# A perceiver block on one core: ternary weights turned by DMA, the first rounds and the tail re-ordered

## The chip, the core and the metric

The kernel runs on one core of a Trainium2 chip. TensorE multiplies, VectorE (DVE) and ScalarE (ACT) read its results out of PSUM, GpSimd (POOL) works beside them in SBUF, and SyncE (SP) issues the DMAs in order. The metric is the device time of one execution in microseconds. Before the change it is 314.23 (median of 3 runs, 314.06 to 314.25).

## What is computed

Thirty-two sequences of 64 rows of 512 go through three layers: cross attention with low-rank queries and keys (16 heads, latent width 32), self attention with one head of 128, and a feed-forward layer whose activations are quantized to 4 bits after a Hadamard transform and whose weights are ternary.

```python
x = x + xattn(layernorm(x), ctx, Wq_d, W_qk, Wkv_d, Wv_u)
x = x + attn(layernorm(x), Wqkv, bqkv, Wo, bo)
h = layernorm(x) @ hadamard
s = clip(max(abs(h), -1), 1e-5) / 7            # one step per row
q = clip(round(h / s), -8, 7) * s
scale = clip(mean(abs(w), 1), 1e-5)            # one per output
t = where(w / scale > 0.5, 1, where(w / scale < -0.5, -1, 0)) * scale
x = x + q @ t.T
```

## The kernel before

Two sequences make a pair of 128 rows; there are 16 pairs (0 to 15, N = 15). The work is a software pipeline written out by hand: `body(i, ...)` of each engine does, in round i, the front of pair i+1 (latents, queries, keys, scores), the cross attention of pair i, the self attention of pair i-1 and the feed-forward layer of pair i-2. Rounds -1 to 3 and 12 to 14 are written out, rounds 4 to 11 are a loop, and pairs 13 to 15 end in a tail with an order of its own. Each engine runs its list in the order in which it is written, and waits on semaphores: `made` counts what TensorE has made, `read` what has been read out of PSUM, `done` what VectorE, ScalarE and GpSimd have done. SyncE's list of DMAs is in order too, so a DMA that waits holds those behind it.

The names that matter here:

- `prob`: exponentials of the scores (ACT L385), from `nmx`, the negated maxima (VectorE `largest`, L614 and L618, one call for each half of the heads). TensorE turns them (L957), ScalarE copies them to `prob_t`.
- `latents` copies the latents of the next pair out of PSUM (ScalarE); the projections read them. `x2n` is the normalized input of self attention (GpSimd L314), turned at L1038 and copied to `x2t`; L1046 projects two pairs' queries at once, L1074 and L1078 make queries, keys and values, L1097 the second scores, whose maximum is `second_max` (L644).
- `x3` is turned, copied to `x3t` and multiplied with the Hadamard matrix (L1009) into bank B4. `amax`, `step_raw`, `qinv`, `z` and `qi` quantize that; `qi` are the codes. In the rounds they are turned by a DMA (`codes_by_dma`, behind a small DMA called `gate`), in the tail by TensorE (`quantized_turned`), and `clipped` writes them to `qi_t`. L1156 multiplies them with `tern_t`, VectorE makes `prod`, GpSimd adds `x3` and SyncE stores `res`.
- The ternary weights: `weight_sizes` sums a block of rows' sizes (L585), `weight_scales` makes the thresholds, `ternary(c)` makes block c of `tern` in two operations (L603 `w_neg`, L605). `ternary_transposed` turns two blocks at a time on TensorE (L946), and `ternary_copy` takes them out of PSUM into `tern_t`. Blocks 0 to 2 are made in round 1, block 3 in round 2, and both halves are turned in round 2.
- `keep_busy(n, bank)` issues n matmuls whose result nobody reads. `x2b` is `x2` plus a constant row (GpSimd L328). `hadamard_centred` takes the mean off the Hadamard matrix on GpSimd in round 1.

## Time and profile before

| what | value |
|---|---|
| median of 3 runs | 314.23 us (314.06 to 314.25) |
| the profiled execution, its own time | 315.06 us |
| its span, first to last instruction | 313.3 us |
| mean granted TensorE clock | 0.991 |
| busy: PE, DVE, ACT, POOL | 299.5, 246.9, 208.1, 90.0 us |
| chain that ended last | PE 74%, DVE 11%, ACT 6%, DMA 3% |

The table is of one execution on the profiler. Busy time is an average over stages; the chain of work that ended last says at each place which engine the end waited for. A matmul of 32-bit numbers is recorded as two passes, so a count of passes is twice that of the code's matmuls.

### The profile page before, as it was taken

What the parts mean: (1) busy time and instruction counts of PE and PEld (TensorE: products, weight loads), DVE (VectorE), ACT (ScalarE), POOL (GpSimd) and SP (SyncE); (2) the same over time, 40 slices, a digit from 0 to 9 for tenths busy, and PEclk for the clock granted to TensorE, in tenths of its full rate; (3) what the DMA queues carried; (4) which work ended last, traced back from release to release, by engine and by line L of the source; (5) the groups of instructions that cost most, each with busy time, mean ns of one, the idle gap of its engine ahead of it and who ended that gap; (6) DMA issues with size and microseconds to landing.
All of it is one profiled execution on the core that took longest, in us unless ns stands there. A gap on an engine that the chain in (4) does not pass through costs nothing.

```text
span 313.3 us, 8324 instructions
## 1 busy us (share of the span) xinstructions
PE 299.5 (96%) x3043; PEld 207.5 (66%) x3058; DVE 246.9 (79%) x530; ACT 208.1 (66%) x587; POOL 90.0 (29%) x130
## 2 busy tenths in 40 slices
PE   7997989999999999999999999999999999999993
PEld 6754857667576766768576766768576866648642
DVE  1689798887879878887879878887879878896366
ACT  2578478768596676768596676768596777784400
POOL 2008304140323324051323324051323324141411
PEclk9999799999999999999999999999999999999998
DMA  7995002051311603041310603051311102000001
GB/s 216 376 363 187 4 8 96 19 189 31 106 49 36 186 1 134 17 157 61 108 43 33 184 0 134 17 173 44 110 43 63 26 0 69 19 35 2 33 0 67
DMA packets 20968, 26.94 MB, mean 86 GB/s; under 512 B 10704, under 2 KB 11472, under 8 KB 20944
## 3 DMA queue, kind: packets, MB, share of 16 engines
q1 hardware_dynamic: 20944, 26.62, 26.1%
q8 instruction: 15, 0.25, 0.4%
q14 instruction: 9, 0.07, 0.1%
HBM read 20.71 MB, written 4.19 MB: 80 GB/s over the span
## 4 chain that ended last, share of the span: by engine, by line
PE 74%; DVE 11%; ACT 6%; DMA 3%; SPq 2%; issue 2%; POOL 0%; DVEq 0%; POOLq 0%
PE ps L1009 10%; PE ps L1074 9%; PE ps L957 7%; PE ps L1132 5%; PE ps L1112 4%; PE ps L1078 4%; PE ps L1162 4%; ACT prob L385 4%; PE ps L967 3%; PE ps L1185 3%; PE ps L1156 3%; DMA bo_row<-bo 3%; PE ps L1046 3%; PE ps L1030 2%; DVE mx L614 2%
## 5 line engine op out<-in xcount | busy, mean ns | idle before, releaser
L385 ACT ACTIVATE prob<-ps,nmx,qk_scale 128x128 f32<-128x128 f32 x240 | 89.8, 469 | 34.9 <-DVE nmx L618 34.9
L1009 PE MATMUL ps<-had_s,x3t 128*128 128x512 f32 x104 | 48.2, 605 | 0.7 <-ACT x3t L379 0.7
L614 DVE TENSOR_REDUCE mx<-ps 128x8 f32<-128x1024 f32 x31 | 37.7, 1217 | 7.0 <-PE ps L1132 7.0
L334 POOL TENSOR_TENSOR qk_scale<-aux,power 128x1 f32<-128x1 f32 x16 | 9.3, 580 | 98.4 <-DVE aux L636 98.4
L623 DVE TENSOR_REDUCE sum_a<-prob 128x8 f32<-128x1024 f32 x30 | 35.8, 1210 | 0.0
L379 ACT ACTIVATE prob_t<-ps 128x512 f32<-128x512 f32 x63 | 34.8, 622 | 0.7 <-PE ps L957 0.3
L1009 PEld LDWEIGHTS ps<-had_s,x3t 128*128 128x128 f32 x104 | 18.6, 190 | 24.5 <-issue 22.7
L957 PE MATMUL ps<-ident,prob 128*128 128x128 f32 x240 | 31.8, 276 | 2.1 <-ACT prob L385 2.1
L957 PEld LDWEIGHTS ps<-ident,prob 128*128 128x128 f32 x240 | 26.6, 141 | 5.5 <-ACT prob L385 4.7
L1074 PE MATMUL ps<-x2t,wqkv_s 128*128 128x128 f32 x224 | 28.6, 281 | 0.4
L1074 PEld LDWEIGHTS ps<-x2t,wqkv_s 128*128 128x128 f32 x224 | 26.1, 192 | 2.2 <-ACT x2t L379 1.3
L338 POOL TENSOR_TENSOR res<-prod,x 128x512 f32<-128x512 f32 x13 | 16.5, 1271 | 34.1 <-DVE prod L769 34.1
L1132 PE MATMUL ps<-ckv,q_t 32*64 32x128 f32 x1024 | 19.2, 278 | 0.2 <-ACT ckv L379 0.2
L967 PEld LDWEIGHTS ps<-wv_bd,u_t 128*128 128x128 f32 x112 | 14.6, 192 | 6.9 <-issue 6.2
L311 POOL TENSOR_TENSOR rstd<-aux,power 128x1 f32<-128x1 f32 x14 | 7.7, 548 | 36.7 <-DVE aux L666 36.7
L328 POOL TENSOR_TENSOR x2b<-x,const_row 128x512 f32<-128x512 f32 x14 | 17.8, 1272 | 0.0
L1132 PEld LDWEIGHTS ps<-ckv,q_t 32*64 32x64 f32 x1024 | 15.5, 131 | 2.8 <-issue 0.8
L1112 PE MATMUL ps<-prob_t,ckv_k 128*32 128x256 f32 x240 | 16.1, 385 | 0.3 <-ACT prob_t L379 0.3
L967 PE MATMUL ps<-wv_bd,u_t 128*128 128x128 f32 x112 | 14.8, 276 | 0.5 <-ACT u_t L379 0.5
L1078 PE MATMUL ps<-wqkv_s,x2t 128*128 128x128 f32 x112 | 14.8, 275 | 0.0
L379 ACT ACTIVATE x2t<-ps 128x512 f32<-128x512 f32 x16 | 9.6, 599 | 7.6 <-PE ps L1038 7.2
L1162 PE MATMUL ps<-wo_s,o2t 128*128 128x512 f32 x28 | 14.3, 592 | 0.0
(200 smaller groups left out, 577.1 us busy)
## 6 DMA issues: line engine op xcount, KB each, us to landing
ct<-ctx_cols SPq DMA_DIRECT2D x16, 512.0 KB, 4.8
xt<-x_cols SPq DMA_DIRECT2D x16, 256.0 KB, 2.9
xr<-x_rows SPq DMA_DIRECT2D x16, 256.0 KB, 4.2
y<-res SPq DMA_DIRECT2D x15, 256.0 KB, 2.0
had_s<-hadamard SPq DMA_DIRECT2D x1, 1024.0 KB, 7.7
w_rows<-weight SPq DMA_DIRECT2D x1, 1024.0 KB, 10.7
wqkv_s<-wqkv SPq DMA_DIRECT2D x1, 768.0 KB, 8.4
wqk<-w_qk SPq DMA_DIRECT2D x2, 128.0 KB, 4.3
```

Source lines behind the costliest of these rows:

```text
L379: return nc.scalar.activation(dst, src, ACT.Copy)
L385: last = nc.scalar.activation(prob[:, h, :], ps[:, h // 4, (h % 4) * P:(h % 4) * P + P], ACT.Exp, bias=nmx[:, h:h + 1], scale=qk_scale[:])
L614: V.tensor_reduce(mx[:, h], ps[:, 2 * half:2 * half + 2, :].rearrange("p r (c k) -> p (r c) k", c=EC), AX.X, ALU.max).then_inc(done["mx"], 1)
L623: V.tensor_reduce(sum_a[:, h], prob[:, h, :], AX.X, ALU.add).then_inc(done["sum"], 1)
L957: mm = pe.transpose(ps[:, r, c * P:(c + 1) * P], prob[:, 4 * r + c, :], ident[:])
L967: mm = pe.matmul(ps[:, B1, c * P:(c + 1) * P], u_t[:, c, :], wv_bd[:, c, :], start=True, stop=True)
L1009: mm = pe.matmul(ps[:, B4, :], x3t[:, c, :], had_s[:, c, :], start=(c == 0), stop=(c == EC - 1))
L1074: mm = pe.matmul(ps[:, B1, s * P:(s + 1) * P], wqkv_s[:, c, s * P:(s + 1) * P], x2t[:, c, :], start=(c == 0), stop=(c == EC - 1))
L1078: mm = pe.matmul(ps[:, B2, 0:P], x2t[:, c, :], wqkv_s[:, c, 2 * P:3 * P], start=(c == 0), stop=(c == EC - 1))
L1112: mm = pe.matmul(ps[32 * r:32 * r + 32, B2, :].rearrange("p (c t) -> p c t", c=EC) [:, :, 64 * bb:64 * bb + 64], ckv_k[:, bb, :], prob_t[: ...
L1132: mm = pe.matmul(ps[64 * bb:64 * bb + 64, r, c * P:(c + 1) * P], q_t[g, 1 - par, bb, c, :], ckv[g, 1 - par, bb * SKV:(bb + 1) * SKV], star ...
L1162: pe.matmul(ps[:, B3, :], o2t[:], wo_s[:], start=True, stop=True).then_inc(made["wo"], 1)
```

## The change

- The blocks of `tern` are turned by four DMAs into `tern_t` (`ternary_by_dma`), two issued in round 1 and two in round 2 behind the codes of pair 0. TensorE's transposes and ScalarE's copies of them are gone, and TensorE waits for all four DMAs before the first integer product.
- Round 0 and 1 on VectorE: the last `weight_sizes` moves behind pair 0's second normalization, `ternary(1)` moves ahead of `second_max`, and `ternary(2)` goes to round 2, ahead of `amax`.
- Round 1 on ScalarE and TensorE: `latents` moves behind the exponentials, and six idle-filling matmuls stand ahead of the second half's transposes. Three more are at the start.
- Tail: pair 13's codes are clipped ahead of `second_max`, and its integer product stands ahead of x2's turning, with one filling matmul in place of three. The codes of pair 15 are made, turned and clipped in two halves; `quantizer` is the part of `quantized` ahead of z, with a name of its own.

```diff
+            def ternary_by_dma(c):
+                sp.wait_ge(tern_done, c + 1)
+                sp.dma_start(tern_t[:, :, c * P:(c + 1) * P], tern[:, c, :], transpose=True).then_inc(ternary_turned, 16)
...
+                if pre and 1 <= i <= 2:
+                    for c in range(2):
+                        ternary_by_dma(2 * i - 2 + c)
...
-                if front and not (isinstance(i, int) and i == 0):
+                if front and not (isinstance(i, int) and 0 <= i <= 1):
                     latents()
-                if isinstance(i, int) and i == 2:
-                    ternary_copy(0, B1)
...
+                    if isinstance(i, int) and i == 1:
+                        latents()
...
-                if isinstance(i, int) and i == 2:
-                    ternary_copy(1, 0)
...
                     largest(1, 0)
-                    weight_sizes(3, EC)
                     largest(1, 1)
                 if first and i == 1:
+                    weight_sizes(3, EC)
                     output_bias()
...
                     ternary(0)
                     sums(1)
                     second_query()
+                    ternary(1)
                     second_max()
                     row_variance()
                     row_scale()
-                    ternary(1)
-                    ternary(2)
...
+                    if first and i == 2:
+                        ternary(2)
...
             second_variance(N)
+            clipped(N - 2, B4)
             second_max(N - 1, B3)
-            clipped(N - 2, B4)
             second_sum(N - 1)
...
-            quantized(N, 3, amax_n, floor3_n, step_n, qinv_n)
+            quantizer(N, 3, amax_n, floor3_n, step_n, qinv_n)
+            after(dve, made["qit"], 1)
+            for h in range(2):
+                cols = slice(h * E // 2, (h + 1) * E // 2)
+                V.tensor_scalar(z[:, cols], ps[:, 3, cols], qinv_n[:], ROUND, ALU.mult, ALU.add).then_inc(half_z, 1)
+                dve.wait_ge(half_z, h + 1)
+                V.tensor_scalar(qi[:, cols], z[:, cols], ROUND, QMAX, ALU.subtract, ALU.min).then_inc(half_codes, 1)
             V.tensor_scalar(qscale_n[:], step_n[:], rstd3_n[:], None, ALU.mult).then_inc(done["qscale"], 1)
-            clipped(N, 2)
+            after(dve, made["int"], N - 1)
+            for h in range(2):
+                dve.wait_ge(half_turned, h + 1)
+                V.tensor_scalar(qi_t[:, 2 * h:2 * h + 2],
+                                ps[:, (2, B2)[h], :].bitcast(BF16)[:, 0:E // 2].rearrange("p (c t) -> p c t", c=2),
+                                QMIN, None, ALU.max).then_inc(half_clipped, 1)
             scaled(N - 1)
...
-            keep_busy(1, 0)
+            keep_busy(2, 0)
...
-                        keep_busy(1, 0)
+                        keep_busy(3, 0)
...
-                        if first and i == 2 and c == 0:
-                            pe.wait_ge(read["xo"], 2)
-                            ternary_transposed(0, B1)
...
+                    keep_busy(6, B3)
...
-                if first and i == 2:
-                    pe.wait_ge(read["pt"], i * 4 + 1)
-                    ternary_transposed(1, 0)
...
                 if quant:
+                    if first and i == 2:
+                        pe.wait_ge(ternary_turned, 16 * EC)
                     after(pe, read["qit"], i - 2)
...
             second_scores(N - 1, B3)
-            keep_busy(3, B1)
-            x2_turned(N, 2)
             after(pe, read["qit"], N - 2)
             for c in range(EC):
                 mm = pe.matmul(ps[:, B4, :], qi_t[:, c, :], tern_t[:, c, :], start=(c == 0), stop=(c == EC - 1))
             mm.then_inc(made["int"], 1)
+            keep_busy(1, B1)
+            x2_turned(N, 2)
             p2_turned(N - 1, B3)
...
-            quantized_turned(N, 2)
-            keep_busy(1, B1)
-            after(pe, read["qit"], N)
+            for h in range(2):
+                pe.wait_ge(half_codes, h + 1)
+                for c in range(2):
+                    mm = pe.transpose(ps[:, (2, B2)[h], :].bitcast(BF16)[:, c * P:(c + 1) * P],
+                                      qi[:, (2 * h + c) * P:(2 * h + c + 1) * P], ident_b[:])
+                mm.then_inc(half_turned, 1)
+                keep_busy(1, B1)
             for h in range(2):
                 for c in range(EC):
+                    if h == 0 and c % 2 == 0:
+                        pe.wait_ge(half_clipped, c // 2 + 1)
```

VectorE at the end of round 1, before: from the second scores' maximum of pair 0, behind the copy of the next queries, to the maximum of pair 2's first scores. In brackets stands what an operation waits for.

```order
L644 TENSOR_REDUCE mx<-ps 128x1 [waits made_s2]
L646 TENSOR_SCALAR nmx<-mx 128x1 [waits done_mx2]
L628 BN_STATS stat<-xr 128x6 [waits made_lat,ld_xr0]
L631 BN_AGGR mv<-stat 128x2 [waits done_stat1,ld_wq]
L636 TENSOR_SCALAR aux<-mv 128x1 [waits done_qk_scale,done_mv1]
L603 TENSOR_SCALAR w_neg<-w_rows,w_nhalf 128x512 [waits tern_done,whalf_done]
L605 SCALAR_TENSOR_TENSOR tern<-w_rows,w_half,w_neg 128x512 [waits neg_done]
L603 TENSOR_SCALAR w_neg<-w_rows,w_nhalf 128x512 [waits tern_done,whalf_done]
L605 SCALAR_TENSOR_TENSOR tern<-w_rows,w_half,w_neg 128x512 [waits neg_done]
L747 RECIPROCAL rsum<-sum_a 128x16 [waits done_xm,done_sum]
L751 RECIPROCAL rsum<-sum 128x1 [waits done_exp2]
L614 TENSOR_REDUCE mx<-ps 128x8 [waits made_s]
```

And after:

```order
L604 TENSOR_SCALAR w_neg<-w_rows,w_nhalf 128x512 [waits tern_done,whalf_done]
L606 SCALAR_TENSOR_TENSOR tern<-w_rows,w_half,w_neg 128x512 [waits neg_done]
L645 TENSOR_REDUCE mx<-ps 128x1 [waits made_s2]
L647 TENSOR_SCALAR nmx<-mx 128x1 [waits done_mx2]
L629 BN_STATS stat<-xr 128x6 [waits made_lat,ld_xr0]
L632 BN_AGGR mv<-stat 128x2 [waits done_stat1,ld_wq]
L637 TENSOR_SCALAR aux<-mv 128x1 [waits done_qk_scale,done_mv1]
L749 RECIPROCAL rsum<-sum_a 128x16 [waits done_xm,done_sum]
L753 RECIPROCAL rsum<-sum 128x1 [waits done_exp2]
L615 TENSOR_REDUCE mx<-ps 128x8 [waits made_s]
```

Block 1 (w_neg and tern) has moved ahead of the second scores' maximum, and block 2 has left this place.

VectorE in round 2, around the quantizer's maximum, before and then after:

```order
L712 TENSOR_SCALAR aux<-mv 128x1 [waits done_mv3]
L715 TENSOR_REDUCE amax<-ps 128x1 [waits made_had]
L603 TENSOR_SCALAR w_neg<-w_rows,w_nhalf 128x512 [waits tern_done,whalf_done]
L605 SCALAR_TENSOR_TENSOR tern<-w_rows,w_half,w_neg 128x512 [waits neg_done]
L722 TENSOR_SCALAR step_raw<-amax,floor 128x1 [waits done_floor3,done_amax]
```

```order
L712 TENSOR_SCALAR aux<-mv 128x1 [waits done_mv3]
L604 TENSOR_SCALAR w_neg<-w_rows,w_nhalf 128x512 [waits tern_done,whalf_done]
L606 SCALAR_TENSOR_TENSOR tern<-w_rows,w_half,w_neg 128x512 [waits neg_done]
L717 TENSOR_REDUCE amax<-ps 128x1 [waits made_had]
L604 TENSOR_SCALAR w_neg<-w_rows,w_nhalf 128x512 [waits tern_done,whalf_done]
L606 SCALAR_TENSOR_TENSOR tern<-w_rows,w_half,w_neg 128x512 [waits neg_done]
L724 TENSOR_SCALAR step_raw<-amax,floor 128x1 [waits done_floor3,done_amax]
```

Block 2 now stands between aux and amax, block 3 where it stood.

SyncE from the rows of pair 2 to the first store, before and then after:

```order
L219 DMA xr<-x_rows 128x512 [waits read_xo]
L215 DMA ct<-ctx_cols 128x1024 [waits made_lat]
L219 DMA xr<-x_rows 128x512 [waits read_xo]
L223 DMA gate<-bqkv 16x1 [waits done_qi]
L224 DMA_TRANSPOSE codes<-qi 128x4x128
L228 DMA y<-res 128x512 [waits done_res]
```

```order
L220 DMA xr<-x_rows 128x512 [waits read_xo]
L224 DMA_TRANSPOSE tern_t<-tern 128x4x128 [waits tern_done] x2
L216 DMA ct<-ctx_cols 128x1024 [waits made_lat]
L220 DMA xr<-x_rows 128x512 [waits read_xo]
L228 DMA gate<-bqkv 16x1 [waits done_qi]
L229 DMA_TRANSPOSE codes<-qi 128x4x128
L224 DMA_TRANSPOSE tern_t<-tern 128x4x128 [waits tern_done] x2
L233 DMA y<-res 128x512 [waits done_res]
```

Blocks 0 and 1 are turned behind the rows' load of round 1, and blocks 2 and 3 behind the codes.

## Rows read from the trace of the kernel before

**Rows 1.** Windows of 1 us: window, length, busy time by engine, granted clock, DMA.
```profile
30.00:31.00 1.00, 0.39 (x4) 0.39 (x5) 0.97 (x6) 1.00 (x4) 0.58 (x3) 1.00 1.00 395
...
33.00:34.00 1.00, 1.00 (x10) 1.00 (x12) 0.96 (x2) 1.00 (x3) 0.72 (x1) 0.50 0.00 0
```

**Rows 2.** Timeline of TensorE, round 1: start, length, operation, idle before.
```profile
30.61 1.21 PE L957 MATMUL ps<-ident,prob 128*128 128x128 f32 x8 [2.08 <-ACT prob L385]
31.79 1.12 PE L1038 MATMUL ps<-ident,x2n 128*128 128x128 f32 x4
32.84 2.08 PE L1046 MATMUL ps<-lat,wqk 64*128 64x128 f32 x16
```

**Rows 3.** Chain that ended last, rounds 2 and 3: start, length, what.
```profile
46.49 1.10 PE ps L1009 x2
47.59 0.45 PE ps L946 x8
...
72.90 1.09 PE ps L1046 x16
```

**Rows 4.** Timeline, end of round 1 (VectorE, and TensorE's scores of pair 2).
```profile
38.11 0.23 DVE L644 TENSOR_REDUCE mx<-ps 128x1 f32<-128x64 f32 x1 [2.11 <-PE ps L1097]
...
39.54 0.49 DVE L603 TENSOR_SCALAR w_neg<-w_rows,w_nhalf 128x512 f32<-128x512 f32 x1
...
39.89 1.20 PE L1132 MATMUL ps<-ckv,q_t 32*64 32x128 f32 x64
...
40.06 0.75 DVE L605 SCALAR_TENSOR_TENSOR tern<-w_rows,w_half,w_neg 128x512 bf16<-128x512 f32 x1
...
42.30 1.21 DVE L614 TENSOR_REDUCE mx<-ps 128x8 f32<-128x1024 f32 x1
```

**Rows 5.** Timeline, round 2 (VectorE and ScalarE).
```profile
44.41 0.68 DVE L651 TENSOR_TENSOR xm<-ps,rsum 128x512 f32<-128x512 f32 x1
...
48.07 1.02 ACT L379 ACTIVATE tern_t<-ps 128x1024 bf16<-128x1024 bf16 x1 [0.48 <-PE ps L946]
...
49.59 0.15 DVE L712 TENSOR_SCALAR aux<-mv 128x1 f32<-128x1 f32 x1
...
50.70 0.69 DVE L715 TENSOR_REDUCE amax<-ps 128x1 f32<-128x512 f32 x1 [0.97 <-PE ps L1009]
...
51.31 1.01 DVE L603 TENSOR_SCALAR w_neg<-w_rows,w_nhalf 128x512 f32<-128x512 f32 x1
...
54.25 0.43 DVE L729 TENSOR_SCALAR qi<-z 128x512 bf16<-128x512 f32 x1
...
57.09 0.30 ACT L472 ACTIVATE p<-ps,nmx 64x64 f32<-64x64 f32 x1
```

**Rows 6.** The codes' transposing DMA (timeline, and view of tile codes), and TensorE's integer product.
```profile
55.10 1.30 SPq L224 DMA_TRANSPOSE codes<-qi  x1
...
60.43 0.81 PE L1156 MATMUL ps<-tern_t,qi_t 128*128 128x512 bf16 x3
```
```profile
L224 SPq DMA_TRANSPOSE codes<-qi x13: 1188/1195/1297, 55.1 to 266.4; - x13
...
DMA to landing us min/median/max: 2.4/2.4/2.5
```

**Rows 7.** Timeline of the tail.
```profile
288.80 0.60 ACT L379 ACTIVATE x2t<-ps 128x512 f32<-128x512 f32 x1 [0.35 <-PE ps L1168]
...
289.57 1.06 PE L1202 MATMUL ps<-x2t,wqkv_s 128*128 128x128 f32 x8
...
305.84 0.75 DVE L821 TENSOR_SCALAR z<-ps,qinv_n 128x512 f32<-128x512 f32 x1
...
307.54 0.42 DVE L830 TENSOR_SCALAR qi_t<-ps 128x512 bf16<-128x512 bf16 x1 [0.37 <-PE ps L1168]
...
308.71 1.26 POOL L364 TENSOR_TENSOR res<-prod,x 128x512 f32<-128x512 f32 x1 [8.18 <-DVE prod L848]
...
309.29 0.96 DVE L903 TENSOR_TENSOR res<-prod_n,x 128x256 f32<-128x256 f32 x1
...
310.68 0.42 DVE L903 TENSOR_TENSOR res<-prod_n,x 128x256 f32<-128x256 f32 x1
```

25 lines of the change are left out of this document (6 added, 19 removed).

## Prediction

> **What bounds the kernel now.** I read the chain that ended last first, then the engines' timeline of the stretches that the change touches, then granted clock by microsecond. The middle of the kernel is one chain of matmuls, round after round, and nothing in it is touched; so what is won or lost before round 3 is carried to the end unchanged, and the change is worth what it does to rounds 1 and 2 and to the tail. Three things stand in the way there. First, TensorE sits idle for 2.08 us ahead of the second half of pair 1's transposes [rows 2], and then its granted clock is 0.50, the lower of its two levels (1.2 GHz against 2.4), where it had been 1.00 [rows 1]: the paired projection's 16 passes take 2.08 us there and 1.09 in round 3 [rows 2, 3]. Second, VectorE makes two ternary rows at 39.54 to 42.2, one at 40.06 and another behind it, and so starts the maximum of pair 2 at 42.30, although the scores that it reads (1.20 us from 39.89) had ended at 41.09 [rows 4]. Third, round 2 has the ternary weights' transposes in TensorE's row ahead of the last Hadamard passes, ScalarE's copy of them (1.02 us, once for each half), and a VectorE that waits 0.97 us for the Hadamard product and only then makes the last ternary row [rows 5].
>
> **Round 1, clock.** Six more idle-filling matmuls (0.11 us for each of their twelve passes, about 1.3 us) fall into the gap of 2.08 us. ScalarE does the copy of the latents behind the exponentials rather than between them, so these end some 0.4 us sooner; the gap that is left is about 0.4 us. The gap that brought the clock down was five times that, so I take the clock to stay at its upper level. The turning of x2 still waits for GpSimd, since GpSimd's work ahead of it is untouched; it starts at 31.79 as before [rows 2]. From there: four transposes at full clock, about 0.45; the projection 1.09 instead of 2.08; then queries, keys, values in 2.8. The second scores would be there at about 36.4 instead of 38.1, 1.7 us sooner.
>
> **Round 1, VectorE.** Its row is serial up to the copy of the queries; what follows had waited 2.11 us when it started at 38.11 [rows 4], so the copy ended at 36.0; the weight size moved to behind aux2 takes 0.68 us there, but the same amount is swallowed where the first comparison (w_neg) waited for GpSimd's x2b, so I take 0 for it (at worst 0.68 later). Behind the queries now comes ternary row 1: 0.49 + 0.75 + 0.03 between them [rows 4] = 1.27, to 37.3. The second scores' maximum started at 38.11 [rows 4] and can start at 37.3: 0.81 sooner, with TensorE no longer what it waits for. The two exponentials, the ckv copy and the scores of pair 2 follow: 39.89 - 0.81 = 39.1, end 40.3. VectorE has no ternary row left there, is free at 38.8, and takes the maximum at 40.3 instead of 42.30: 2.0 us gained. What is late next is that wait for the scores.
>
> **Round 2.** The six exponentials and x3's copy follow that maximum: the Hadamard product starts at 46.49 - 2.0 = 44.5 [rows 3]. It loses the eight transposes that stood in it (0.45) and so has ended by 48.2, not 50.7. VectorE, however, gains less: its next operations wait for the output and attended matmuls behind the scores, which came only 0.81 sooner, so xm moves from 44.41 to 43.1 (1.3) [rows 5], and with it all that follows on VectorE and GpSimd; aux3 ends at 49.74 - 1.3 = 48.4 [rows 5]. Ternary row 2 now goes into the place of the 0.97 us wait: 1.27, to 49.7; amax 0.69, to 50.4. The comparison of row 3 took 1.01 us instead of 0.49 because x2b held it [rows 4, 5]; x2b is 1.3 sooner too, so it ends 1.3 sooner, and the codes (qi) end at 54.68 - 1.3 = 53.4.
>
> The shared lock shows in the rows: 1.01 against 0.49 of the same comparison [rows 4, 5], and in the tail 0.96 against 0.42 [rows 7]. The Trainium skill (SBUF — State Buffer, "SBUF: two separate sides") says the same, that VectorE and GpSimd share one port pair, held by one of them for a whole instruction; by that rule the 0.68 us of the moved weight size would be hidden as I took it.
>
> **The transposes by DMA, where the forecast is decided.** Ternary rows 0 and 1 go at 34 and 37.3, with over 20 us to spare. Rows 2 and 3 stand in SyncE's queue behind the codes of pair 0, so they can't leave before qi is done, although the rows themselves are ready at 49.7 and 51.8. Codes: issue at 55.10 - 1.3 = 53.8, 1.30 us on the queue, 2.4 us to landing [rows 6]. If each one follows as soon as the queue has issued the one ahead, the third is issued at 53.8 + 2.6 = 56.4 and lands at 58.8. The integer product needs it; it started at 60.4 [rows 6]. TensorE by itself would be there at 58.35: the codes end at 53.4, the sums take 1.2, the second maximum 0.4, so the exponentials of p start at 55.05 instead of 57.09 [rows 5], 2.05 sooner; the copy of the ternary halves (1.02 each) is gone from ScalarE, so it is not in the way. So the landing is last, by 0.45, and the product starts at 58.8: **1.6 us gained**. No row shows a transposing DMA queued behind another. Its price lies between the 1.2 to 1.3 us of an issue and the 2.4 us of a whole one [rows 6]; I take 1.3, since the destination engines were busy for only half a microsecond of the 2.4. The two ends give 58.35 (TensorE's own) and 61.0.
>
> A rule speaks against the edit. The Trainium skill (VectorE: DVE Perf Modes, "Rules for kernel authors") says to transpose a 128x128 block on TensorE if PSUM will do, and its table "The three transpose paths" prices the DMA path at 1309 ns for a block of bfloat16. These instructions turn four blocks each; by that price, added up, three of them would take 15.7 us and end at 69.5. The trace disagrees: four blocks land in 2.4.
>
> **Tail.** Pair 13's integers are made ahead of x2's turning. The matmuls then fall where three filling ones stood, but the queries of pair 15 wait for ScalarE's copy of x2t anyway, 288.80 + 0.60 = 289.40 against a start at 289.57, with one weight load of 0.1 before it [rows 7]: 0.05 gained. The last codes in halves: z, at 305.84, takes 0.75 whole; a half can't take under 0.38 and I estimate 0.48, and 0.30 for half of the 0.43 of qi [rows 5, 7]. Four half steps and their hand-overs end at 307.39, where the whole codes ended at 307.05. The transposes of the second half are two instead of four, and the second clip ends at about 308.04 instead of 307.96 [rows 7]. The product of pair 14 stands behind it, GpSimd's sum behind that (from 308.71, 1.26 us) and the end behind GpSimd: the first half of the last sum takes 0.96 instead of 0.42 and ends 0.28 after GpSimd [rows 7]. So the end moves by +0.08. The integer matmuls gain nothing. Both together: 0.03 later, bounds -0.2 and +0.4. The start's filling matmuls lie in waits for loads: 0.
>
> **Sum.** The profiled execution took 315.06 (span 313.3, 1.76 around it). 315.06 - 1.6 + 0.03 = 313.5. The median of the runs lies 0.83 under the profiled one: 312.7.
>
> **Rivals.** (a) The transposes are not what comes last, because they queue closer than 1.3 us or qi is sooner: product at 58.35, gain 2.05: 312.2. For it: the DMA engines are hardly busy. Against: the issue alone is 1.2 to 1.3. (b) The clock falls all the same, at 31.5: then the second maximum stays at 38.11 and the scores of pair 2 at 39.89; only the ternary row behind it is gone, 1.2 us at the maximum, 0.5 at xm and about 0.5 at qi, third landing at 59.6: gain 0.8, 313.5. For it: filling leaves a gap of 0.4 and another of 0.4 ahead of x2. (c) The gain is swallowed before round 3 by a wait not seen here, such as VectorE's longer row: 314.2. (d) Slower: each transposing DMA waits until the one ahead has landed. Then the third lands at 53.8 + 3 x 2.4 = 61.0, 0.6 later than the product started, and the tail adds its 0.03: 314.9. It decides from a spacing of 2.1 us on ((60.4 - 2.4 - 53.8) / 2). Against it: the DMA engines' short work in each.
>
> **How the numbers follow.** Forecast 0.53, (a) 0.17, (b) 0.12, (c) 0.10, (d) 0.08. A difference under 0.2% (0.63 us) is about what a measurement of this kernel can't tell from none; (b) lies on the near side of that line for two parts in three. Faster 0.79, same 0.13, slower 0.08. The range goes from (a) with a little of the tail's bound, 311.9, to beyond (b), 313.9; (d) and half of (c) are left out.
>
> **What would show it.** Granted clock 1.00 from 28 to 36 us; second maximum at 37.3; maximum of pair 2 at 40.3; qi of pair 0 ending at 53.4; three transposing DMAs 1.3 us apart and TensorE waiting for the last some 0.4 us before the integer product at 58.8; rounds 3 on in the same lengths as before; the last sum still held by GpSimd. I am wrong if the clock falls, if the third transposing DMA lands later than 60.4, or if VectorE's row in round 1 isn't done by 37.3.

## The result: slower by 0.6%

| version | median, us | lowest to highest | runs |
|---|---|---|---|
| before | 314.24 | 313.55 to 315.74 | 20 |
| changed | 316.08 | 314.55 to 318.01 | 20 |

The ratio is 1.0059, with a 95% interval of 1.0039 to 1.008. The forecast was 312.7 with a range up to 313.9, so it is wrong in sign and by 3.4 us. The runs of the changed kernel spread over 3.5 us, those of before over 2.2. The spread of the changed kernel has a pattern: ten of the twenty executions have a mean granted TensorE clock of 0.993 or less and a median of 317.6, the other ten have 0.996 or more and a median of 315.0. The profiled one took 317.7 and is of the first ten, so it shows a loss of 2.6 us where the medians show 1.8.

The profiled execution has a span of 315.9 (before 313.3) and a mean granted clock of 0.992 (before 0.991): there is again one fall of the clock, but in another place. Place by place, along the steps of the prediction:

**Start.** TensorE's timeline of the changed kernel, then that of the kernel before (start, length, engine, line, operation, count). The passes of the same code take 1.81 instead of 1.22, and the first scores come 2.4 us later; a part of it are the added fillers.

```profile
0.98 2.93 PE L925 MATMUL ps<-mean_w 128*128 128x128 f32 x12 [0.98 <-POOL power L293]
...
3.70 1.81 PE L932 MATMUL ps<-wq_raw,mean_w 128*128 128x64 f32 x8
...
9.03 1.08 PE L1003 MATMUL ps<-ct,wkv_s 128*32 128x256 f32 x8
...
12.46 1.20 PE L1130 MATMUL ps<-ckv,q_t 32*64 32x128 f32 x64 [0.17 <-ACT ckv L387]
```
```profile
3.70 1.22 PE L916 MATMUL ps<-wq_raw,mean_w 128*128 128x64 f32 x8
...
7.08 0.64 PE L996 MATMUL ps<-ct,wkv_s 128*32 128x256 f32 x8 [0.52 <-DMA ct<-ctx_cols]
...
10.06 1.20 PE L1132 MATMUL ps<-ckv,q_t 32*64 32x128 f32 x64 [0.17 <-ACT ckv L379]
```

By the maximum of pair 1's first scores (24.19, before 22.91) 1.28 us of that is left. So the times of rounds 1 and 2 are compared from there. (VectorE's first `weight_sizes` stands ahead of this maximum in both kernels; the moved one stands behind it.)

**Round 1.** The changed kernel again: TensorE, the windows that answer to [rows 1], and VectorE.

```profile
30.52 1.50 PE L925 MATMUL ps<-mean_w 128*128 128x128 f32 x12
31.86 1.04 PE L964 MATMUL ps<-ident,prob 128*128 128x128 f32 x8
32.84 0.65 PE L1042 MATMUL ps<-ident,x2n 128*128 128x128 f32 x4
33.42 1.16 PE L1050 MATMUL ps<-lat,wqk 64*128 64x128 f32 x16
```
```profile
30.00:31.00 1.00, 1.00 (x12) 1.00 (x11) 1.00 (x4) 1.00 (x5) 1.00 (x2) 1.00 0.81 301
33.00:34.00 1.00, 1.00 (x14) 0.83 (x15) 1.00 (x1) 0.47 (x1) 1.00 (x2) 1.00 0.68 262
```
```profile
38.13 0.22 DVE L645 TENSOR_REDUCE mx<-ps 128x1 f32<-128x64 f32 x1
...
41.14 1.23 DVE L615 TENSOR_REDUCE mx<-ps 128x8 f32<-128x1024 f32 x1 [1.31 <-PE ps L1130]
```

The six fillers fill the gap, the clock stays at 1.00, and the paired projection's 16 passes take 1.16 where [rows 2] has 2.08. The second scores' maximum starts at 38.13 with no idle time before it: VectorE's own row is what it waited for, as forecast. The maximum of pair 2 starts at 41.14, before 42.30 [rows 4]: 1.16 sooner by the clock on the wall, 2.44 counted from the late start.

**Round 2.** VectorE, SyncE's queue, then the chain that ended last, in the changed kernel and in the kernel before.

```profile
51.03 1.13 DVE L604 TENSOR_SCALAR w_neg<-w_rows,w_nhalf 128x512 f32<-128x512 f32 x1
...
54.09 0.43 DVE L731 TENSOR_SCALAR qi<-z 128x512 bf16<-128x512 f32 x1
```
```profile
54.93 1.19 SPq L229 DMA_TRANSPOSE codes<-qi  x1
56.16 2.58 SPq L224 DMA_TRANSPOSE tern_t<-tern  x2
```
```profile
57.47 3.77 DMA tern_t<-tern
61.25 0.05 issue
61.29 1.52 PE ps L1156 x4
62.81 1.71 PE ps L1162 x2
64.52 1.24 PE ps L974 x8
...
67.79 3.63 PE ps L1016 x8
```
```profile
60.43 0.81 PE ps L1156 x3
61.24 0.86 PE ps L1162 x2
62.10 0.89 PE ps L967 x8
...
65.20 3.63 PE ps L1009 x8
```

The last step of the codes starts at 54.09, before 54.25 [rows 5], and ends at 54.52 (before 54.68). The three transposing DMAs are issued at 54.93, 56.16 and 57.47, 1.2 and 1.3 apart, as forecast. The third lands 3.8 us after its issue and not 2.4, at 61.24. TensorE waits for it and then runs the next three groups in 4.47 instead of 2.56 us (one of the four passes of before's integer product isn't in its record):

```profile
61.29 1.52 PE L1156 MATMUL ps<-tern_t,qi_t 128*128 128x512 bf16 x4 [2.17 <-DMA tern_t<-tern]
```
```profile
60.00:61.00 1.00, 0.00 (x0) 0.00 (x0) 0.14 (x1) 0.82 (x3) 0.00 (x0) 1.00 0.06 7
61.00:62.00 1.00, 0.71 (x3) 0.36 (x4) 0.00 (x0) 1.00 (x4) 0.00 (x0) 0.85 0.00 0
62.00:63.00 1.00, 1.00 (x3) 0.68 (x2) 0.15 (x1) 0.38 (x2) 0.00 (x0) 0.50 0.00 0
```

The granted clock was 1.00 through the wait and is 0.50 from 61.7 to 65.1 us. The next Hadamard product starts at 67.79 instead of 65.20. That is 2.59 us, the spans differ by 2.6, and the groups of rounds 3 to 13 have the same lengths as before (the 96 Hadamard passes 605 ns each in both).

**Tail.** VectorE and GpSimd of the changed kernel; the rows answer to [rows 7].

```profile
308.41 0.48 DVE L900 TENSOR_SCALAR z<-ps,qinv_n 128x256 f32<-128x256 f32 x1
...
311.36 1.26 POOL L372 TENSOR_TENSOR res<-prod,x 128x512 f32<-128x512 f32 x1 [8.26 <-DVE prod L853]
311.72 1.18 DVE L919 TENSOR_TENSOR res<-prod_n,x 128x256 f32<-128x256 f32 x1
...
313.33 0.42 DVE L919 TENSOR_TENSOR res<-prod_n,x 128x256 f32<-128x256 f32 x1
```

From z to the start of the last sum it is 4.92; [rows 7] has 4.84. The last sum is still held by GpSimd's.

### The profile page after: what moved, and what is told of

It is laid out like the page before. It is cut to its first block, busy times and chain, and to the rows that moved or that the text cites. A ratio compares the mean times of both kernels' runs of the same rounds, so it can differ in the third digit from the quotient of the medians.

```text
span 315.9 us, 8341 instructions
## 1 busy us (share of the span) xinstructions
PE 303.7 (96%) x3058; PEld 210.1 (67%) x3058; DVE 247.3 (78%) x533; ACT 206.0 (65%) x585; POOL 90.1 (29%) x130
## 4 chain that ended last, share of the span: by engine, by line
PE 76%; DVE 16%; ACT 3%; issue 2%; DMA 1%; SPq 1%; DVEq 0%; POOL 0%; POOLq 0%
PE ps L1016 9%; PE ps L1077 7%; PE ps L964 6%; PE ps L1130 5%; PE ps L1162 4%; PE ps L1112 4%; PE ps L974 4%; PE ps L1156 4%; PE ps L1185 3%; PE ps L1081 3%; DVE mx L615 3%; PE ps L1034 3%; PE ps L1050 2%; PE ps L925 2%; PE ps L996 2%
## 5 line engine op out<-in xcount | busy, mean ns | idle before, releaser
L1156 PE MATMUL ps<-tern_t,qi_t 128*128 128x512 bf16 x52 | 13.8, 390 | 2.2 <-DMA tern_t<-tern 2.2
L1162 PE MATMUL ps<-wo_s,o2t 128*128 128x512 f32 x28 | 15.2, 626 | 0.0
```

Of the source, the lines that this page charges most:

```text
L1156: mm = pe.matmul(ps[:, B4, :], qi_t[:, c, :], tern_t[:, c, :], start=(c == 0), stop=(c == EC - 1))
L1162: pe.matmul(ps[:, B3, :], o2t[:], wo_s[:], start=True, stop=True).then_inc(made["wo"], 1)
```

## First experiments: which part costs the time

The changed kernel loses in three places that were not foreseen (start, landing, clock). The theories when the first four versions ran: A, the start's fillers delay everything; B, the ternary DMAs queued behind the codes and the wait that they make.

### The start's fillers taken back

```diff
-            keep_busy(2, 0)
+            keep_busy(1, 0)
...
-                        keep_busy(3, 0)
+                        keep_busy(1, 0)
```

> The changed kernel, with the idle-filling matmuls of the start as they were before (1 and 1 in place of 2 and 3). Theory A: at the start TensorE's matmuls ran at the slower pace in the changed kernel's profile (the first eight of the mean in 1.81 us, 1.22 before), and the added fillers, twice as long there, held the first context matmuls from 7.1 to 9.0; without them those start at about 7.1 to 8.0 and the time falls by about 1.3, to 314.8, with less spread. Rival: the pace of the start differs from run to run by itself, the fillers hold nothing, and the time stays at 316.1 with its spread of 3.5 us.

316.52 (314.82 to 317.37, ratio 1.0039, 1.0015 to 1.0062). Nothing is gained. Its third transposing DMA lands 3.6 after the issue, TensorE waits 2.03 and its product takes 1.81 at the lower clock, much as in the changed kernel.

### Only the start's fillers, in the kernel before

```diff
-            keep_busy(1, 0)
+            keep_busy(2, 0)
...
-                        keep_busy(1, 0)
+                        keep_busy(3, 0)
```

> The kernel before, with only the fillers of the start added (2 and 3). Theory A: part of the runs get 1 to 2 us longer, median about 315.3, and the context matmuls start at up to 9.0. Rival (my prediction's step, the fillers lie in waits for loads): 314.2, context matmuls at 7.1.

315.06 (313.82 to 315.95, ratio 1.0007, 0.9984 to 1.0029): no difference that can be told. The first scores are 2.1 us later (12.19), yet the next Hadamard product starts at 64.84, 0.4 sooner than before. In this profile the late start is given back in round 1, where the gap is shorter and no fall follows:

```profile
31.88 1.10 PE L957 MATMUL ps<-ident,prob 128*128 128x128 f32 x8 [1.47 <-ACT prob L385]
```

That is one execution. Six of the twelve have a mean granted clock of 0.992 or less, and so have 13 of the 31 of before beside them, so the fillers don't keep the fall away. They aren't needed for a late start either: the profile of the version with only the tail, whose start is that of before, has its first scores at 11.38, a gap of 1.48 and no fall.

### Ternary blocks 2 and 3 ahead of the codes

Everything else is as in the changed kernel.

```diff
-                if quant and (not pre or i < PAIRS - 1):
-                    codes_by_dma(i - 2)
                 if pre and 1 <= i <= 2:
                     for c in range(2):
                         ternary_by_dma(2 * i - 2 + c)
+                if quant and (not pre or i < PAIRS - 1):
+                    codes_by_dma(i - 2)
```

> The changed kernel, with the transposing DMAs of ternary blocks 2 and 3 ahead of the codes of pair 0 in SyncE's queue. Theory B: the 2.4 us wait ahead of round 2's integer product, and the clock's fall behind it (int, output and attended matmuls in 1.52, 1.71, 1.24 instead of 0.86, 0.86, 0.91 by the chain, some 1.8 us), are both due to the place in the queue; both go, the product starts 2.4 us sooner, and the time falls by about 4, to 312.2. Rival: a transposing DMA of this shape lands late wherever it stands, or the codes behind two of them land late; then the product still waits 1 us or more, and the time falls by under 2.

313.01 (312.75 to 313.91, ratio 0.994, 0.9917 to 0.9964): 3.1 us less than the changed kernel and faster than before. SyncE's queue and TensorE:

```profile
50.56 3.62 SPq L224 DMA_TRANSPOSE tern_t<-tern  x2
```
```profile
58.99 1.03 PE L1156 MATMUL ps<-tern_t,qi_t 128*128 128x512 bf16 x4
```

No wait, no fall, and the Hadamard product starts at 63.97 (changed kernel 67.79). From pair 1's first maximum to that product it is 39.75 us against 43.60: 3.85 less in this pair of profiles, 3.1 in the medians (the two were not run side by side). The whole loss, and the gain that the prediction summed, hang on these two DMAs' place in the queue. Theory B stands, theory A falls.

### Only the tail, in the kernel before

```diff
+            clipped(N - 2, B4)
             second_max(N - 1, B3)
-            clipped(N - 2, B4)
...
-            quantized(N, 3, amax_n, floor3_n, step_n, qinv_n)
+            quantizer(N, 3, amax_n, floor3_n, step_n, qinv_n)
...
+            for h in range(2):
...
+                V.tensor_scalar(z[:, cols], ...)
...
+                V.tensor_scalar(qi[:, cols], ...)
```

(with the halves' transposes and clips, as in the change)

> The kernel before with only the tail's two edits (pair 13's integers sooner, pair 15's codes in halves). By my sum: +0.03, so 314.2 to 314.3. In the changed kernel's profile the sum of pair 15's first half took 1.18 instead of 0.96 and the end lay 9.1 us behind the Hadamard product's last maximum where it had been 8.6 or so; by that reading it is +0.4: 314.6. Rival: the halves gain what they are for, -0.3: 313.9.

314.9 (313.61 to 315.97, ratio 0.9997, 0.9976 to 1.0019). From z to the last sum it is 4.92 against 4.84: the halves cost 0.08, as summed. From round 3's Hadamard product to that z it is 240.68 against 240.64, so pair 13's integers move nothing above 0.04.

## Second group: the clock's share, and which parts are worth keeping

### Queue order and start

The version with blocks 2 and 3 ahead, and the start's fillers taken back as above.

```diff
-                        keep_busy(3, 0)
+                        keep_busy(1, 0)
```

> The changed kernel with blocks 2 and 3 ahead of the codes in SyncE's queue, and the start's fillers as before (1 and 1). In the profiles with a slow start the first scores came at 11.4 with the old fillers and at 12.2 to 12.5 with the added ones, and at 10.1 with an early rise of the clock. Theory A (the fillers are a cost only where the clock is late): 0.8 to 1 less than with them where the start is slow, more where it is early; median about 312.0. Rival: VectorE's row of rounds 0 and 1 swallows what the start gains; 313.0 as with the fillers.

312.85 (312.28 to 314.56, ratio 0.9949, 0.9926 to 0.9972): the same as with the fillers.

### The wait filled

The changed kernel, with ten fillers ahead of the wait for the ternary DMAs.

```diff
+                    after(pe, read["qit"], i - 2)
                     if first and i == 2:
+                        keep_busy(10, B4)
                         pe.wait_ge(ternary_turned, 16 * EC)
-                    after(pe, read["qit"], i - 2)
```

> The changed kernel with ten idle-filling matmuls (20 passes, some 2.1 us) into bank B4 just ahead of the wait for the transposing DMAs in round 2. Theory B in two parts: the wait of 2.2 us stays, the clock no longer falls, and the int, output and attended matmuls take 0.86, 0.86, 0.9 again by the chain: 1.6 to 1.9 less than the changed kernel's 316.1, so 314.4, granted clock 1.00 from 60 to 66. Rival: the fall has another cause than the idle stretch, the clock still shows 0.50 behind it, and the time stays at 316.

315.1 (314.76 to 316.32, ratio 1.0024, 1.0008 to 1.0041): 1.0 less than the changed kernel in the median. TensorE:

```profile
58.61 2.40 PE L925 MATMUL ps<-mean_w 128*128 128x128 f32 x20
61.38 0.81 PE L1157 MATMUL ps<-tern_t,qi_t 128*128 128x512 bf16 x3 [0.37 <-DMA tern_t<-tern]
```

The DMA lands as late as ever (4.0), but the clock stays at 1.00, and from the product to the Hadamard product it is 4.76 us instead of 6.50 (before 4.77). So of the loss 1.7 us is the lower clock behind the wait in this pair of profiles, and the wait itself is the rest. The other executions agree: none of these twelve has a mean granted clock under 0.997, where ten of the changed kernel's twenty have 0.993 or less, and their median, 315.1, is that of its other ten (315.0). So the wait alone costs about 2.1 us (against 313.0 without it). The fall comes on top in half of the executions, which is why it moves the median by only 1 us.

### Round 1 without the six fillers

The version with blocks 2 and 3 ahead.

```diff
-                    keep_busy(6, B3)
```

> The queue-mended kernel without the six fillers of round 1 (start's fillers kept). My prediction's step: these hold the clock up; without them it falls behind the gap of some 1.5 us in part of the runs, and the second scores come 1 us or more later there: median +0.5, spread wider, up to 315. Rival: the gap alone, now shortened by the latents' copy behind the exponentials, doesn't bring the clock down, VectorE is last in round 1 anyway, and the time stays at 313.0.

313.33 (312.21 to 314.14, ratio 0.996, 0.9941 to 0.9978): no difference that can be told from 313.01. In the profile the gap is 1.70 and no fall follows (three of the twelve executions have a mean granted clock of 0.994; where in them it fell no trace shows):

```profile
30.67 1.09 PE L964 MATMUL ps<-ident,prob 128*128 128x128 f32 x8 [1.70 <-ACT prob L393]
```

### The tail of before

The version with blocks 2 and 3 ahead.

```diff
-            quantizer(N, 3, amax_n, floor3_n, step_n, qinv_n)
...
+            quantized(N, 3, amax_n, floor3_n, step_n, qinv_n)
...
+            clipped(N, 2)
```

> The queue-mended kernel with the tail as it was before. From the last z's start to the last sum's start the profiles show 4.84 us with the old tail and 4.92 with the new one, and 1.14 against 1.10 of gain between round 3 and that z: 0.1 less with the old tail, 312.9. Rival: the halves pay, 313.3.

312.82 (312.47 to 313.74, ratio 0.9944, 0.9926 to 0.9963): the tail's edits are worth nothing.

### One block ahead, one behind

The changed kernel with block 2 ahead of the codes.

```diff
+                if pre and i == 2:
+                    ternary_by_dma(2)
                 if quant and (not pre or i < PAIRS - 1):
                     codes_by_dma(i - 2)
-                if pre and 1 <= i <= 2:
-                    for c in range(2):
-                        ternary_by_dma(2 * i - 2 + c)
+                if pre and i == 1:
+                    ternary_by_dma(0)
+                    ternary_by_dma(1)
+                if pre and i == 2:
+                    ternary_by_dma(3)
```

> The changed kernel with block 2 ahead of the codes in the queue and block 3 alone behind them. Theory C: transposing DMAs queued closely are served one after the other, about 1.9 to 2.0 us each (codes issued at 54.93 plus 2.4, then two more, last landing 61.24), so one alone behind the codes lands about 4.4 us after the codes' issue, 3.2 after its own: integer product at about 59.3, a wait of 0.4 us, no fall of the clock: 313.3. Rival: the spacing of 1.3 us of the issues decides and only a third one in a row is late; then it lands 2.4 after its issue, no wait, 313.0. Other rival: block 3's own landing takes 3.8 wherever it follows the codes: wait 1.2 us, 314.5.

312.85 (312.67 to 313.02, ratio 0.9934, 0.9909 to 0.9959). TensorE doesn't wait. The time between issue and landing of the block behind the codes (issued at 55.08):

```profile
DMA to landing us min/median/max: 2.5/2.5/2.5
```

Second in a row, 1.23 behind the codes (issued at 53.85), it lands as if alone. A queue that serves one after another (theory C) would have given 3.2 or more, so that price was wrong too. Something else holds the third.

### The best parts together

Blocks 2 and 3 ahead, start's fillers and tail as before.

```diff
-                        keep_busy(3, 0)
+                        keep_busy(1, 0)
...
+            quantized(N, 3, amax_n, floor3_n, step_n, qinv_n)
...
```

> The changed kernel with the queue mended, the start's fillers as before and the tail as before: 312.6 to 312.8, no more than 0.2 under the kernels with one of the two. Rival: the two add up with something not seen, 313.3.

313.03 (312.43 to 314.35, ratio 0.9955, 0.9936 to 0.9974): not better than any one of them. Six versions without the late landing lie between 312.8 and 313.3, and their intervals overlap.

### Only round 1's clock, in the kernel before

```diff
-                if front and not (isinstance(i, int) and i == 0):
+                if front and not (isinstance(i, int) and 0 <= i <= 1):
                     latents()
...
+                    if isinstance(i, int) and i == 1:
+                        latents()
...
+                    keep_busy(6, B3)
```

> The kernel before with only round 1's six fillers and the latents' copy behind the exponentials. Theory (my prediction's first step): the fall of the clock in round 1 goes, and the second scores come 1.7 us sooner in a run that had it; but two ternary rows on VectorE follow, its row was last by 1.2 us at pair 2's maximum, so no more than 0.5 to 0.6 is gained at the end: 313.8. Rival: the fall is there in few runs, and nothing changes: 314.4.

314.12 (313.6 to 315.2, ratio 0.998, 0.9962 to 0.9998). The clock stays up in round 1 (in the profile, which is the slowest of the twelve, it falls at the start instead, from 9.3 to 12.8 us), and that alone is worth at most 0.4% in the median. From pair 1's first maximum to pair 2's it is 18.02 us here (24.39 to 42.41), 19.39 before and 16.95 in the changed kernel: the rest of round 1's gain comes from the ternary rows moved on VectorE.

But 19.39 is the time of an execution that had the fall. The profiles of the three other versions that keep before's rounds 1 and 2 (start only, tail only, longer start) had none, without any edit there, and they have 18.02 to 18.03 as well. All times from pair 1's first maximum, in us:

| profiles | second scores' maximum | pair 2's maximum | codes end | next Hadamard product |
|---|---|---|---|---|
| before, clock fell in round 1 | 15.20 | 19.39 | 31.77 | 42.29 |
| four versions with before's order of work, no fall | 13.82 to 13.83 | 18.02 to 18.03 | 30.40 to 30.41 | 40.92 to 40.93 |
| changed kernel | 13.94 | 16.95 | 30.33 | 43.60 |
| six versions without the late landing, and three in a row | 13.93 to 13.95 | 16.94 to 16.96 | 30.31 to 30.33 | 39.73 to 39.76 |

The fall costs 1.37 us. Most executions of before don't seem to have it: of the 112 that were run beside the versions, 48 have a mean granted clock of 0.993 or less, with medians of 315.3 to 315.6 in the four groups, and 64 have more, with 313.9 to 314.3. (The mean doesn't say where the clock fell; the profile with the fall has 0.991.) None of the twelve executions here is at 0.993 or less, against 12 of the 30 beside them. So the edit takes the fall away where there would be one, and gives the other executions nothing.

### A longer start, in the kernel before

```diff
-            keep_busy(1, 0)
+            keep_busy(4, 0)
...
-                        keep_busy(1, 0)
+                        keep_busy(6, 0)
```

> The kernel before with 4 and 6 idle-filling matmuls at the start in place of 1 and 1. Theory A: at the slower pace a filler takes 0.53 us (its two passes 0.55 in the changed kernel's profile), at the faster one 0.22, so the first scores come between 11 and 14 and the median is 1 to 2 us over the kernel before, 315.4 to 316.4. Rival: rounds 0 and 1 wait for loads until 18.7 anyway (bo_row in the chain of the kernel before), and under 0.5 comes through.

313.91 (313.52 to 314.8, ratio 0.9976, 0.9959 to 0.9993). Eight more fillers do no harm; the expectation from theory A was the wrong way round. The interval even lies just under 1, and none of the twelve executions has a mean granted clock under 0.996, where 12 of the 30 of before beside them have 0.993 or less. That a late start shortens the gap in round 1 and so keeps the clock up fits this (the gap is 1.48 in this profile, first scores at 11.89), but the three fillers more of the version above didn't do it, so it is argued and not shown.

## Third group: what makes the third transposing DMA late

Two facts of the traces point away from the row of three. First, in the changed kernel the second one lands in 2.5; the third's data move on time and only a trickle is left. This is the view of DMA traffic from 56 to 62 us of the changed kernel: share and GB/s in 40 slices of 0.15 us, and under it the landing of the two ternary blocks.

```profile
DMA  1999820003999610505999998000001000000000
GB/s 27 193 222 218 181 33 0 0 0 68 212 224 212 145 14 0 109 0 108 212 203 205 84 5 0 5 9 10 9 10 16 0 0 0 0 0 0 0 0 0
```
```profile
DMA to landing us min/median/max: 2.5/3.1/3.8
```

Three humps of data (56.2, 57.5, 58.7), 1.3 apart. Ahead of the third stands a single value of 109: a fetch of program code, one packet of 16 KB that begins at 58.54 and takes 1.3 us. Behind the third hump 5 to 16 GB/s go on until 60.7. Second, single transposing DMAs of the codes, far from any other, show the same trickle in some rounds (4.1 us in one round of the version with blocks 2 and 3 ahead, 2.4 in the next). In all the profiles shown so far, each of those that took 2.6 us or more has a fetch of program code in its data or in the microsecond ahead of them. The first block of round 1 does so in every profile that turns it by DMA, 3.1 to 3.4.

The count over all seventeen profiles, those of this group included, is as clear. They have 270 transposing DMAs. In 38 of them a fetch is under way at some time between the issue and 2.0 us behind it: 35 of these landed after 2.6 to 4.4 us, the other three after 2.5 to 2.6. None of the remaining 232 took more than 2.55, and 26 of those have a fetch that begins 2.0 to 2.5 us behind the issue. So what matters is a fetch before or during the moving of the data.

So a new theory, F: the fetch. Its rival, Q: three in a row.

### Two small DMAs ahead of block 3

The version with one block behind, and two copies of 64 bytes between the codes and block 3, which move its data onto the fetch. No three transposing DMAs stand in a row here.

```diff
                 if pre and i == 2:
+                    for j in range(2):
+                        sp.dma_start(spacer[:, j:j + 1], bqkv.rearrange("(s p o) -> s p o", p=P, o=1)[0][0:16]).then_inc(spaced, 16)
                     ternary_by_dma(3)
```

> The version with block 2 of the ternary weights ahead of the codes and block 3 alone behind them, with two small DMAs (64 bytes each, like the gate) put between the codes and block 3. In the version without them block 3 was issued 1.26 us behind the codes, landed 2.5 us later, and its data had moved by 57.2, just ahead of a fetch of program code (16 KB, one packet) that began at 57.44. The two small ones take 0.39 us of the queue each, so that block 3 moves its data at 57.2 to 57.9, across the fetch. Theory F (a transposing DMA whose data comes right behind a fetch of program code lands late, because one engine's share waits for the fetch's packet): block 3 lands 3.1 to 4.0 us after its issue at about 55.9, at 59.0 to 59.9, TensorE waits 0.9 to 1.8 us; 313.6 to 315. Theory Q (what makes the third one late is that three transposing DMAs stand in a row): it lands in 2.5, at 58.4, TensorE waits 0.3: 313.1.

315.56 (314.55 to 317.95, ratio 1.0029, 1.0002 to 1.0056): 2.7 us slower than without the two by the medians, 3.0 by the ratios to the kernel before beside each. SyncE's queue, TensorE, and the landing:

```profile
55.04 1.04 SPq L286 DMA_DIRECT2D spacer<-bqkv  x2
56.12 1.19 SPq L226 DMA_TRANSPOSE tern_t<-tern  x1
```
```profile
60.96 1.49 PE L1164 MATMUL ps<-tern_t,qi_t 128*128 128x512 bf16 x3 [2.96 <-DMA tern_t<-tern]
```
```profile
GB/s 0 0 0 0 0 0 0 0 0 9 182 215 211 39 0 0 1 0 0 0 0 140 209 207 132 7 0 0 0 0 8 10 9 14 3 0 0 0 0 0
...
tern_t<-tern SPq DMA_TRANSPOSE x1, 4.4
```

1.04 us later at its issue, 4.4 instead of 2.5 to the landing, with the same trickle behind (53 to 61 us, slices of 0.2). A row of three is not needed.

### Three in a row, with no fetch near

The version with blocks 2 and 3 ahead, and block 2 turned once more in between, into a spare tile that nobody reads.

```diff
                     for c in range(2):
                         ternary_by_dma(2 * i - 2 + c)
+                        if i == 2 and c == 0:
+                            sp.dma_start(tern_spare[:], tern[:, 2, :], transpose=True).then_inc(spare_turned, 16)
```

> The version with blocks 2 and 3 ahead of the codes, and block 2 turned a second time, into a spare tile that nobody reads, between them. That makes three transposing DMAs in a row, about 1.24 us apart, from 50.6 on, with no fetch of program code near (the nearest at about 47 and 58.9), and the last of the three is block 3. Theory Q (three in a row): block 3 lands 3.6 to 4.0 us after its issue, still in time for the product; time as without the second turning, 313.0. Theory F (the fetch): all three land in 2.4 to 2.5; 313.0 too. The landing decides, not the time.

312.6 (312.44 to 312.99, ratio 0.9929, 0.9893 to 0.9965). They are issued at 49.62, 50.86 and 52.17. The view of DMA traffic from 49 to 55 us:

```profile
tern_t<-tern SPq DMA_TRANSPOSE x2, 2.5
tern_spare<-tern SPq DMA_TRANSPOSE x1, 2.5
```

All three take 2.5. A row of three is not enough either: theory Q falls.

### Five small DMAs ahead of block 3

The version with two small DMAs, with five in their place.

```diff
+                    for j in range(5):
```

> The same as with two small DMAs, but with five: block 3 is issued at about 57.0 and moves its data from 58.4 on, when the fetch of program code that began at 57.44 (1.1 to 1.2 us) is nearly or wholly over. Theory F: block 3 lands in 2.5 to 2.8, at 59.5 to 59.8, so the wait is hardly longer than with two spacers although the issue is 1.15 later; TensorE waits 1.4 to 1.7 us, 314.4 to 315. Theory Q: it lands in 2.5. A third theory, S (the small DMAs themselves delay it): later than with two, 3.5 or more.

318.07 (316.12 to 319.62, ratio 1.0089, 1.0063 to 1.0114). The profile is of the fastest execution, 316.12:

```profile
58.70 1.19 SPq L226 DMA_TRANSPOSE tern_t<-tern  x1
```
```profile
61.45 0.81 PE L1164 MATMUL ps<-tern_t,qi_t 128*128 128x512 bf16 x3 [3.44 <-DMA tern_t<-tern]
```
```profile
tern_t<-tern SPq DMA_TRANSPOSE x1, 2.5
```

The five took 3.60 us of the queue, not 1.95, so block 3 left at 58.70 and the time missed what was expected. The other eight executions, 316.65 to 319.62, have a mean granted clock of 0.988 to 0.993, this one 0.996: they seem to have had a fall as well. The landing didn't: 2.5, behind the fetch (57.26 to 58.30). Same block, same place in the queue, ahead of the fetch 2.5, on it 4.4, behind it 2.5. Theory F stands, and the spacers themselves (theory S) don't delay it.

Why the changed kernel meets the fetch: in its profile and in the two other versions of its order the fetch starts 0.1 us behind TensorE's first matmul with the attention's values (58.42 and 58.53 here), and that matmul and the third DMA both follow from the codes: their last step ends at 54.52, the matmul starts 3.9 us later and the third DMA's data move from 4.2 us later on. In the kernel before, the codes' only DMA has long landed when the fetch comes at 59.6. That the fetch follows that matmul is seen in these profiles and no rule: it starts 0.45 us behind it with blocks 2 and 3 ahead of the codes, and 0.05 ahead of it with five small DMAs. Whose program is fetched no view tells. That the changed kernel's other executions meet it too is likely from their times, none of which is under 314.55, but only profiles show it.

## Why the prediction was wrong, point by point

- **Clock in round 1** (stays up): right. But the fall was one of the profiled execution; 64 of 112 executions of before don't seem to have it, and to them the edit gives nothing. Alone it moves the median by 0.2% (interval to 0.4%).
- **VectorE's row in round 1** (0.81 sooner at the second maximum, 2.0 at pair 2's): right in mechanism; from pair 1's maximum on it was 1.26 and 2.44 sooner than in the profile of before. Against an execution without the fall it is 0.12 later and 1.07 sooner.
- **The codes** (end 1.3 sooner, at 53.4): 54.52. From pair 1's maximum on it is 1.44 sooner, so the size was right for an execution with the fall; the 1.1 us that is missing on the wall is the start (1.28 late). Against executions without the fall it is 0.08.
- **Start's fillers** ("lie in waits for loads: 0"): their place was misread. They stand at TensorE's start, where the pace differs from one execution to the next, and not in waits alone. For the end they are worth nothing that can be told all the same: the changed kernel with and without them, the kernel before with and without them, and the version with the queue mended with and without them. Only the longer start differs, and it is 0.2% faster.
- **Spacing of the DMAs** (1.3): right, 1.23 and 1.31. The reason given, DMA engines busy for half a microsecond of the 2.4, was a low reading: 22% of the 3 us around one such DMA is 0.66 us in the profile of before. It decides nothing.
- **Landing of the third** (2.4 after its issue): the step that failed. It was 3.8, and with it the wait was 2.2 us instead of 0.45. The 2.4 came from thirteen codes' DMAs in one profile [rows 6], none of which met a fetch of program code in its first 2 us; the range knew only the spacing as unknown, from 1.3 to 2.4, not the landing.
- **What the wait does** (nothing): second failure. I had read from [rows 1, 2] that a gap of 2.08 us was followed by the lower clock and did not apply it to the wait that rival (d) would make. The fall costs another 1.7 us in the profile.
- **Rival (d)** named the right place by a wrong mechanism: it put the landing 7.2 us behind the codes' issue, the forecast 5.0, and it was 6.3 (54.93 to 61.24). It missed the clock, and so gave 314.9 instead of 316.1. Its chance of 0.08 was too low for a DMA whose price was taken from one row of its kind.
- **Tail** (+0.03): the halves cost 0.08, as summed.
- **The sum itself**: with the two DMAs ahead of the codes the landing is out of the way and the kernel takes 312.8 to 313.3, with 313.01 1.5 us less than the 314.46 of before beside it; the forecast was 1.5. That this agrees is luck. The steps were priced on an execution with the fall, and against it the gain is 2.5 us (39.75 for 42.29 up to the Hadamard product); against one without it is 1.2 (40.92), and the median of before lies between such executions. The 0.83 us between the profiled execution and the median was carried over as if it had nothing to do with the change, though part of it was this fall, which the change takes away. The order of two queue entries was worth 3.1 us.

## What to carry to other kernels

A DMA whose landing is awaited needs slack for a late one, not just for its usual time: put it ahead of what it doesn't depend on in its queue, as soon as its data are ready. Before a gain is read off one profile, see from the granted clock of the other executions whether the profiled one is typical: here it held 1.4 us that most of the others didn't. Before a new wait of 2 us on TensorE is accepted, price the clock behind it too, and if it can't be moved, fill it. When a landing differs from its twins, look at the traffic in the microsecond ahead of it, fetches of program code included, before blaming the queue.

## What the runs showed that was not expected

- **A fetch of program code delays a transposing DMA.** One packet of 16 KB takes 0.9 to 1.6 us; a transposing DMA of 128x512 bfloat16 whose data come right behind it or with it lands 2.6 to 4.4 us after its issue in 35 of 38 cases, instead of 2.4 to 2.5. Its bulk moves at the usual 200 GB/s and the last tenth or so at about 10 GB/s. That one of the 16 DMA engines is held by the packet would fit these rates; no view here tells the engines apart, so it is argued and not shown. The Trainium skill has two sentences that bear on it: Runtime: NRT & Kernel Launch, "Instruction fetch mechanics", says that each engine refills its program memory in blocks of 16 KiB by a DMA queue of its own, and DMA: Bandwidth & Descriptors, "Queues, rings and completion order", that a DMA engine changes between queues only behind a whole packet. The packets of 16 KB in the traces agree with the first, and with the second the numbers above would follow; neither page says what a fetch costs the DMA behind it, which is up to 2.0 us here.
- **The start's pace is not the same each time.** The same eight passes at 3.7 us took 1.08 to 1.81 us in different profiles; the first scores came at 9.7 to 12.6 us. The windows of the view print a granted clock of 1.00 there each time, but the traces have no record of the clock that early: the record begins, at 1.00, at 3.9 us in one profile and as late as 10.6 in another. Where it begins at 3.85, 4.15, 4.27, 4.91 and 5.16, the eight passes took 1.08, 1.22, 1.28, 1.58 and 1.71; where it begins at 5.4 or later, 1.81. And the first twelve filling passes take 2.93 us, in both kernels, where twelve take 1.50 in round 1. So TensorE ran at the lower of its two levels until then, worked out from these lengths; why it rises 3.9 us into one execution and 10.5 into the next, where (in the changed kernel) TensorE had been busy without a gap since 0.98, stays open.
- **A gap isn't always followed by a fall.** Gaps of 1.47, 1.48 and 1.70 us were not, those of 2.03, 2.08 and 2.17 were, in that of 2.96 the clock fell 0.3 us before it ended, and one of 3.44 in the profile with five small DMAs was not: its product took 0.81 for three passes, at full pace. Seven of the other eight executions of that kernel have a mean granted clock of 0.991 or 0.993, as the profiles with a fall have, and one 0.988. At the start, a gap of 1.01 was followed by a fall (only round 1's clock, at 9.3 us) and one of 0.98 was not (the best parts together). So the length of the gap alone doesn't decide.
- **The small DMAs' price.** One of 64 bytes took 0.34 us of the queue, two 1.04, five 3.60.
